# One block-diagonal matrix per tile instead of two 64-row multiplications on TensorE

## The reference

```python
# x: (B=128, C=128, T=1024) f32; itok_B_0_7: (128,) i32 in 0..7; weights: (8, C=128, D=128) f32
w = weights[subjects]                        # (B, C, D)
out = jnp.einsum('bct,bcd->bdt', x, w)       # per batch: w.T @ x
x = x + out
```

## Time and profile before

| | before |
|---|---|
| median of the runs | 323.58 us |
| the profiled execution, its own time | 323.66 us |
| its span, first to last instruction | 321.7 us |
| PE busy | 249.0 us (77%), 1024 matmul records |
| DVE busy | 196.3 us (61%) |
| ACT busy | 132.3 us (41%) |
| mean granted TensorE clock | 0.892 of full |
| DMA | 134.82 MB, mean 419 GB/s |

### The profile page before, as it was taken

The page is one execution under the profiler, slowest core; times in us unless marked ns, Lnnn a source line. Parts: engine busy times, 40 slices in busy tenths (PEclk is TensorE's granted clock), DMA queues, the critical chain, the costliest instruction groups (busy, mean ns, idle before and its releaser), DMA issues.

```text
span 321.7 us, 2829 instructions
## 1 busy us (share of the span) xinstructions
PE 249.0 (77%) x1024; PEld 114.8 (36%) x1024; DVE 196.3 (61%) x261; ACT 132.3 (41%) x131; POOL 0.8 (0%) x7
## 2 busy tenths in 40 slices
PE   0698929888975969969597796978949599599920
PEld 0343504344432424434242342434414244244410
DVE  3386843868781682838648186483836828368740
ACT  4064622636460552526336063362524525255630
POOL 1000000000000000000000000000000000000000
PEclk9999978999996996979989597797989979699975
DMA  7999999999999999999999999999999999999996
GB/s 287 420 403 430 421 428 428 430 423 427 432 428 425 429 430 426 427 429 429 426 430 429 427 427 428 430 427 428 429 429 426 428 430 427 427 428 429 428 426 259
DMA packets 17590, 134.82 MB, mean 419 GB/s; under 512 B 672, under 2 KB 1200, under 8 KB 1200
## 3 DMA queue, kind: packets, MB, share of 16 engines
q1 hardware_dynamic: 9008, 67.63, 50.1%
q10 hardware_dynamic: 8576, 67.12, 49.3%
HBM read 67.64 MB, written 67.11 MB: 419 GB/s over the span
## 4 chain that ended last, share of the span: by engine, by line
DMA 68%; PE 25%; DVE 2%; issue 1%; DVEq 0%; SPq 0%; ACTq 0%
DMA x_ring<-x 42%; DMA out<-x_ring 26%; PE product L233 25%; DVE x_ring L154 1%; DVE x_ring L153 0%; DVEq L54 0%; SPq L94 0%; DVEq L141 0%; ACTq L202 0%
## 5 line engine op out<-in xcount | busy, mean ns | idle before, releaser
L233 PE MATMUL product<-x_ring,weight_ring 64*128 64x512 f32 x1024 | 249.0, 646 | 59.0 <-DMA x_ring<-x 45.9
L233 PEld LDWEIGHTS product<-x_ring,weight_ring 64*128 64x128 f32 x1024 | 114.8, 206 | 192.3 <-issue 154.9
L153 DVE TENSOR_TENSOR x_ring<-product,x_ring 64x1024 f32<-64x1024 f32 x64 | 77.9, 1217 | 104.6 <-PE product L233 104.6
L196 ACT COPY x_ring<-product 64x1024 f32<-64x1024 f32 x64 | 64.5, 1008 | 173.5 <-PE product L233 173.5
L154 DVE TENSOR_TENSOR x_ring<-product,x_ring 64x1024 f32<-64x1024 f32 x64 | 78.6, 1228 | 0.8
L197 ACT COPY x_ring<-product 64x1024 f32<-64x1024 f32 x64 | 64.2, 1003 | 0.8
L141 DVE COPY weight_ring<-weight_bank 64x256 f32 x128 | 36.9, 288 | 3.9 <-issue 1.0
L188 ACT COPY weight_bank<-weight_halves 64x1024 f32<-64x1024 f32 x2 | 2.2, 1112 | 2.2 <-DMA weight_halves<-weights 2.2
L158 DVE TENSOR_SCALAR subject_row<-subject_row 1x128 int32<-1x128 int32 x1 | 0.2, 215 | 3.7 <-DMA subject_row<-subjects 3.7
L122 DVE COPY weight_bank<-weight_halves 64x1024 f32<-64x1024 f32 x2 | 1.4, 688 | 0.9 <-DMA weight_halves<-weights 0.9
L188 ACT ACT_TABLE_LOAD x1 | 1.3, 1283 | 1.3 <-PEq L249 1.3
## 6 DMA issues: line engine op xcount, KB each, us to landing
x_ring<-x SPq DMA_DIRECT2D x14, 4096.0 KB, 29.8
out<-x_ring ACTq DMA_DIRECT2D x13, 4096.0 KB, 29.5
x_ring<-x SPq DMA_DIRECT2D x4, 2048.0 KB, 16.6
out<-x_ring ACTq DMA_DIRECT2D x6, 1024.0 KB, 11.2
out<-x_ring ACTq DMA_DIRECT2D x3, 2048.0 KB, 16.9
weight_halves<-weights SPq DMA_DIRECT2D x1, 512.0 KB, 4.0
subject_row<-subjects ACTq DMA_DIRECT2D x1, 8.0 KB, 2.9
```

Source lines behind the costliest of these rows:

```text
L153: dve.tensor_tensor(x_ring[LOW, slot, 0, :], low[LOW, :], x_ring[LOW, slot, 0, :], add)
L196: act.copy(x_ring[LOW, slot, 1, :], low[HIGH, :])
L233: last = pe.matmul(product[slot % PRODUCTS][a][:, cols], weight_ring[half, slot, r, :], x_ring[half, slot, r, cols], start=r == 0, stop=r ...
```

## The change

PE multiplies a whole tile, both batches, with 128x128 matrices of two 64x64 blocks on the diagonal: the first batch's block on partitions 0 to 63 and output columns 0 to 63, the second's on partitions and columns 64 to 127, and zeros elsewhere. For each (r, q) there is one such matrix, so there are 8 matmuls per tile as before, each of 128 rows, without a tile position. `product` is one tile of 128 partitions x 2 x 1024 per turn; row q of it is laid out as row r of the x slot. One DVE operation per tile adds it to x; ACT copies nothing and only issues the stores. `eye` and its additions are gone; POOL writes the zeros once into the off-diagonal blocks of `weight_ring`, which now has 8 slots. The diff without declarations of semaphores and other small lines:

```diff
-            pool.memset(eye[:, :], 0.0).then_inc(eye_zero, 1)
-            pool.wait_ge(eye_zero, 1)
-            for begin, made in ((0, eye_low), (H, eye_high)):
-                half = slice(begin, begin + H)
-                pool.affine_select(eye[half, :], eye[half, :], pattern=[[-1, H]], base=0, channel_multiplier=1,
-                                   compare_op=mybir.AluOpType.not_equal, fill=1.0).then_inc(made, 1)
+            pool.memset(weight_ring[LOW, :, :, :, H:D], 0.0).then_inc(zeros_low, 1)
+            pool.memset(weight_ring[HIGH, :, :, :, 0:H], 0.0).then_inc(zeros_high, 1)
...
-                for subject, half in zip(numbers, (LOW, HIGH)):
-                    done = dve.tensor_copy(weight_ring[half, slot, :, :], weight_bank[half, bass.ds(subject, 1), :, :])
+                for subject, half, columns in zip(numbers, (LOW, HIGH), (slice(0, H), slice(H, D))):
+                    done = dve.tensor_copy(
+                        weight_ring[half, slot, :, :, columns],
+                        weight_bank[half, bass.ds(subject, 1), :, :].rearrange("h s r (q k) -> h (s r) q k", q=R))
...
-                dve.tensor_tensor(x_ring[LOW, slot, 0, :], low[LOW, :], x_ring[LOW, slot, 0, :], add)
-                dve.tensor_tensor(x_ring[HIGH, slot, 1, :], high[HIGH, :], x_ring[HIGH, slot, 1, :], add).then_inc(summed, 1)
+                dve.tensor_tensor(x_ring[:, slot, :, :], product[slot % PRODUCTS][:, :, :], x_ring[:, slot, :, :],
+                                  add).then_inc(summed, 1)
...
-            dve.wait_ge(eye_low, 1)
             dve.wait_ge(bank_low, 1)
-            add_eye(LOW, 1, ODD)
-            dve.wait_ge(eye_high, 1)
             dve.wait_ge(bank_high, 1)
-            add_eye(HIGH, 0, EVEN).then_inc(eyes_added, 1)
-            dve.wait_ge(eyes_added, 1)
+            dve.wait_ge(zeros_low, 1)
+            dve.wait_ge(zeros_high, 1)
...
-                act.copy(x_ring[LOW, slot, 1, :], low[HIGH, :])
-                act.copy(x_ring[HIGH, slot, 0, :], high[LOW, :]).then_inc(copied, 1)
...
             for first, count in STORES:
-                for tile in range(first, first + count):
-                    cross(tile, tile % SLOTS)
-                whole(first + count - 1)
+                act.wait_ge(summed, first + count + PRODUCTS)
...
                 pe.wait_ge(summed, tile + 1)
-                pe.wait_ge(copied, tile + 1)
...
-                    for r in range(R):
-                        for a, half in enumerate((LOW, HIGH)):
-                            last = pe.matmul(product[slot % PRODUCTS][a][:, cols], weight_ring[half, slot, r, :],
-                                             x_ring[half, slot, r, cols], start=r == 0, stop=r == R - 1,
-                                             tile_position=(a * H, 0))
+                    for q in range(R):
+                        for r in range(R):
+                            last = pe.matmul(product[slot % PRODUCTS][:, q, cols],
+                                             weight_ring[:, slot % WEIGHT_SLOTS, r, q, :], x_ring[:, slot, r, cols],
+                                             start=r == 0, stop=r == R - 1)
```

More of the change, by code:

```diff
@@ L12 @@
 PRODUCTS = 2
+WEIGHT_SLOTS = 8
 def subject_residual_kernel(nc, x, subjects, weights, out):
@@ L31, in subject_residual_kernel @@
     LAPS = TILES // SLOTS
-    assert TILES % SLOTS == 0 and SLOTS % PLACE == 0 and SLOTS % PRODUCTS == 0 and PICK_AHEAD > PRODUCTS
+    assert TILES % SLOTS == 0 and SLOTS % PLACE == 0 and SLOTS % PRODUCTS == 0
+    assert SLOTS % WEIGHT_SLOTS == 0 and WEIGHT_SLOTS > PICK_AHEAD > PRODUCTS
     PLACES = SLOTS // PLACE
@@ L46, in subject_residual_kernel @@
     LOW, HIGH = slice(0, H), slice(H, C)
-    EVEN, ODD = slice(0, H), slice(H, D)
     EVENS, ODDS = slice(0, S, 2), slice(1, S, 2)
@@ L59, in subject_residual_kernel @@
         weight_bank = ctx.enter_context(nc.sbuf_tensor("weight_bank", [C, S, R, D], f32))
-        weight_ring = ctx.enter_context(nc.sbuf_tensor("weight_ring", [C, SLOTS, R, D], f32))
-        eye = ctx.enter_context(nc.sbuf_tensor("eye", [C, H], f32))
+        weight_ring = ctx.enter_context(nc.sbuf_tensor("weight_ring", [C, WEIGHT_SLOTS, R, R, D], f32))
         subject_row = ctx.enter_context(nc.sbuf_tensor("subject_row", [SUBJECT_ROWS, B], i32))
-        product = [[ctx.enter_context(nc.psum_tensor(f"product{i}_{a}", [D, T], f32)) for a in range(2)]
-                   for i in range(PRODUCTS)]
+        product = [ctx.enter_context(nc.psum_tensor(f"product{i}", [C, R, T], f32)) for i in range(PRODUCTS)]
         subjects_in = ctx.enter_context(nc.semaphore("subjects_in"))
@@ L69, in subject_residual_kernel @@
         weights_in = ctx.enter_context(nc.semaphore("weights_in"))
-        eye_zero = ctx.enter_context(nc.semaphore("eye_zero"))
-        eye_low = ctx.enter_context(nc.semaphore("eye_low"))
-        eye_high = ctx.enter_context(nc.semaphore("eye_high"))
+        zeros_low = ctx.enter_context(nc.semaphore("zeros_low"))
+        zeros_high = ctx.enter_context(nc.semaphore("zeros_high"))
         bank_low = ctx.enter_context(nc.semaphore("bank_low"))
-        eyes_added = ctx.enter_context(nc.semaphore("eyes_added"))
         bank_high = ctx.enter_context(nc.semaphore("bank_high"))
@@ L87, in subject_residual_kernel @@
         summed = ctx.enter_context(nc.semaphore("summed"))
-        copied = ctx.enter_context(nc.semaphore("copied"))
         block = ctx.enter_context(nc.Block())
@@ L124, in bank @@
                     weight_halves[source, :, :, :].rearrange("h i r (k q) -> h i r q k", q=2))
[L126 to L129, removed]
             def subjects_of(tile):
@@ L138, in pick, with total @@
             def pick(slot, numbers):
-                for subject, half in zip(numbers, (LOW, HIGH)):
-                    done = dve.tensor_copy(weight_ring[half, slot, :, :], weight_bank[half, bass.ds(subject, 1), :, :])
-                return done
-            def sums(tile, slot):
-                low, high = product[slot % PRODUCTS]
+                for subject, half, columns in zip(numbers, (LOW, HIGH), (slice(0, H), slice(H, D))):
+                    done = dve.tensor_copy(
+                        weight_ring[half, slot, :, :, columns],
+                        weight_bank[half, bass.ds(subject, 1), :, :].rearrange("h s r (q k) -> h (s r) q k", q=R))
+                return done
+            def total(tile, slot):
                 dve.wait_ge(multiplied, tile + 1)
@@ L176, in _ @@
             for tile in range(TILES):
-                sums(tile, tile % SLOTS)
+                total(tile, tile % SLOTS)
                 ahead = tile + PICK_AHEAD
@@ L182, in _ @@
                     own = ahead % PICK_AHEAD * 2
-                    pick(ahead % SLOTS, numbers[own:own + 2])
+                    pick(ahead % WEIGHT_SLOTS, numbers[own:own + 2])
         @block.scalar
@@ L190, in bank @@
                     weight_halves[source, :, :, :].rearrange("h i r (k q) -> h i r q k", q=2))
-            def cross(tile, slot):
-                low, high = product[slot % PRODUCTS]
-                act.wait_ge(multiplied, tile + 1)
-                act.copy(x_ring[LOW, slot, 1, :], low[HIGH, :])
-                act.copy(x_ring[HIGH, slot, 0, :], high[LOW, :]).then_inc(copied, 1)
-            def whole(tile):
-                act.wait_ge(copied, tile + (PRODUCTS + 1))
-                act.wait_ge(summed, tile + (PRODUCTS + 1))
             act.dma_start(subject_row[:, :], subjects.rearrange("(one b) -> one b", one=1).broadcast_to(
                 (SUBJECT_ROWS, B))).then_inc(subjects_in, DMA_INC)
-            act.sem_inc(copied, PRODUCTS)
             act.wait_ge(weights_in, DMA_INC)
```

## The result

The changed kernel takes 460.32 us (median of 6 runs, 459.58 to 460.63) against 323.58 us before: a ratio of 1.422, 95% interval 1.4202 to 1.4238. The forecast was 460.8 us. The profiled execution has a span of 458.5 us, and 458.8 were forecast.

A forecast was written before the change was run, and what follows sets the result against it. Transfers bound the kernel before, PE the changed one: 9.8 + 1.4 + 439.5 + 0.2 + 2.3 + 0.1 + 5.1 + 0.4 = 458.8 us of span, with 2.0 us around it 460.8 us; range 454 to 472 us.

The forecast's parts named there:

- The term that decides: PE's matmuls: 16 records per tile one by one at 0.429 us, 6.87 us per tile, 439.5 us for 64 tiles.
- the slow start: PE's first four tiles: 15.41 us against 14.00 because PE starts slow; 1.4 us lost again.
- a whole pitch: PE at full clock: the 0.429 us from one pair of 64-row matmul records to the next.
- Rival A: PE: a pair's two matmuls were served one after the other; 322.8 to 323.5 us, chance 6%.
- Rival B: PE: weight loads no longer hide, 0.616 us per record; 652 us, chance 5%.
- What was to hide: Beside PE's 6.87 us per tile: DVE's sum and two copies, 2.9 us; POOL's zeros done by 4.3 us.
- Rival C: PE has gaps, or its clock is lowered under a load without a pause; 475 us and more, chance 3%.
- the prediction's estimate of the limit, 4.67: PE time per tile in us up to which transfers stay the bound, from today's span of PE's start to DVE's last sum.

The follow-up runs named there:

- the run on the same rows: Kernel before, with both matmuls of a pair on rows 0 to 63, reading the first batch's data and matrix; 893.33 us, ratio 2.76.
- the runs with half the matmuls: Kernel after, with half its matmuls left out (r = 1 is not accumulated); 323.3 us, ratio 0.9989.
- two quarters: Kernel after, each 128x128 matmul split into two 64x64 blocks on the array's diagonal quarters, zeros not multiplied, PE's loop unrolled; 459.85 us, ratio 1.4207.
- the runs of four: Kernel before, same matmuls reordered: per tile the first batch's four, then the second's four, instead of in turn; 323.53 us, ratio 0.9999.
- the 4 KB layout: Kernel after, with the tile laid out by whole channels: 128 rows without zeros, transfer pieces of 4 KB instead of 8 KB; 328.1 us, ratio 1.0139.

## Why the prediction was right

**The term that decides** was 439.5 us for 1024 records one by one, and it held; PE was busy for 441.5, of which about 2 are the slow start (forecast 1.4) and the drain. The step under it, that 64-row matmuls run beside each other and each holds its rows a whole pitch, was read from one comparison of durations at two clocks. The runs show it in three ways: single 64-row records 0.43 us apart at full clock, a pair on the same rows at half the rate of a pair on different rows at the same clock, and 0.43 us per added record of 128 rows. Rival A is excluded by these.

**Weight loads.** They last 190 ns and still run within every beat, on the very rows that multiply; PE is busy 13.00 of 13.00 us. Rival B is excluded. A line of the Trainium skill (TensorE: Matmul & The Clock Gate, Part 3, The mechanism) has a weight load overlap only with a matmul on another row group. The loads measured here speak against that line, and the measurement decides. For true fp32 the Trainium skill (FP8 and Floating Point Precision, TensorE Precision Notes) gives four passes through the array. The trace agrees in size with the estimate worked out from them, 0.43 us per record; the passes were not seen one by one.

**What was to hide, hid.** The sum of 2048 numbers takes 2.29 us (2.3 forecast), the copies 0.28; the memsets took 1.80 us each (1.7) and ended long before the bank. PE waited for nothing after its first load, and the clock stayed up (mean 0.995). Rival C did not come. The reason given for the clock, that PE is then never idle, was not enough, though: in the run on the same rows PE was never idle either after its start, and its records kept the duration of 1.2 GHz throughout. That the clock would stay up was right without a reason that the runs bear out.

**Small terms that were off.** PE started at 10.31 us, not 9.8: the first load landed at 10.26, not at 9.73, and was what PE waited for, as forecast. In the runs with half the matmuls and with two quarters the same load ended at 9.41 and 9.86, so it varies from run to run by more than that error. The last store took 3.9 us, not 5.1: it was worked out from two loads at the start, when other loads were under way, and came out too high; that these others are the reason is not shown. The two errors, +0.5 and -1.2, and +0.4 of PE, sum to -0.3 us, by which the span was missed. So the hit within half a microsecond is in part luck: errors of about 1 us cancelled.

**What stays open:** what sets the distance of about two matmuls by which PE runs ahead of the strict order, on which my count for the runs of four rested; why the clock did not rise in the run on the same rows; and what in the 4 KB layout costs the 1.4%.

## What to carry to other kernels

Ask what a matmul occupies, not how much of the array it fills: here a record of 512 streamed columns cost a beat of 0.43 us at full clock whether it used 64 x 64, 64 x 128 or 128 x 128 of the array. (No run varied the number of streamed columns.) Zeros in a block-diagonal matrix cost nothing by themselves, but splitting each batch's 128 output channels over two matmuls streams its data twice. Before two small matmuls are merged, look in the trace whether they already start together; if they do, merging serializes them. And an engine with a quarter of its time free can still become the bound: here 4.04 us of PE per tile stayed hidden behind the transfers and 5.15 did not, with the prediction's estimate of the limit, 4.67, in between; the change needed 6.87.

## What the runs showed of the hardware

- In the run on the same rows, one 64-row matmul at a time throughout, PE stayed at the level of 1.2 GHz for 874 us at 98% busy (records of 1057 ns). One 128-row matmul at a time ran at 2.4 GHz (592 ns, granted 1.00), and so did two 64x64 blocks side by side (589 ns, granted 1.00) and the single 64-row records in the runs of four (589 ns, granted 1.00), which come between pairs.
- The granted clock column read 1.00 in that run; the duration of the records is the safer reading.
- In the runs of four, records on different rows did not keep the strict order: the next run started 1.83 us after the one before it, which lasts 3.43 us.
- An operation on DVE of 0.21 us ended only 0.07 to 0.08 us after POOL's memset had ended, in the kernel after and in the kernel before with the memsets added.
- With pieces of 4 KB instead of 8 KB the transfers moved 422 instead of 428 GB/s in a full stretch, and the kernel took 1.4% longer.
